# Differential attention: keys 0 to 511 of the two softmaxes' addition as an accumulating transfer

## What is computed

```
Q, K = X Wq + bq, X Wk + bk            # 2 x 64 columns a head
A1 = Q1 K1^T / 8 ; A2 = Q2 K2^T / 8    # 1024 x 1024 a head and batch
P  = softmax(A1) - lam * softmax(A2)
O  = P V ;  Y = concat(O) Wo + bo
out = x + 0.2 * layernorm(Y) * gamma + ... + ffn(x)
```

## Time and profile before

| | |
|---|---|
| median of 3 runs | 1207.48 us (1206.95 to 1208.09) |
| the profiled execution | 1207.97 us |
| its span, first to last instruction | 1206.2 us |
| TensorE busy | 1168.2 us, 97% |
| GpSimd busy | 1017.3 us, 84% |
| ScalarE busy | 968.9 us, 80% |
| VectorE busy | 905.6 us, 75% |
| mean granted TensorE clock | 0.99 |
| moved by DMA | 63.41 MB, mean 53 GB/s |

### The profile page before, as it was taken

One profiled execution on the slowest core, in us unless ns is written; L12 is line 12 of the kernel. 1 busy time (PEld: TensorE's weight loads), 2 busy tenths in 40 slices (PEclk: granted clock), 3 DMA queues, 4 the chain that ended last, 5 costly groups with the idle time before them and its releaser, 6 DMA issues.

```text
span 1206.2 us, 28081 instructions
## 1 busy us (share of the span) xinstructions
PE 1168.2 (97%) x9730; PEld 841.2 (70%) x9730; DVE 905.6 (75%) x1573; ACT 968.9 (80%) x1711; POOL 1017.3 (84%) x657
## 2 busy tenths in 40 slices
PE   5899999999999999999999999999999999998998
PEld 4666767666677776767676767676767776765797
DVE  8878878786787878887878887877887877874510
ACT  3398888887888888988888988888888888985432
POOL 3599999999999999999999999999999999989000
PEclk8999999999999999999999999999999999997999
DMA  8832211221112111222221112221112221110000
GB/s 208 312 80 51 50 44 49 49 49 42 23 39 49 49 49 44 49 49 49 49 49 40 30 34 49 49 49 43 49 49 49 49 49 42 25 28 1 1 18 18
DMA packets 74134, 63.41 MB, mean 53 GB/s; under 512 B 45172, under 2 KB 63092, under 8 KB 74100
## 3 DMA queue, kind: packets, MB, share of 16 engines
q1 hardware_dynamic: 73092, 62.78, 20.3%
q10 hardware_dynamic: 880, 0.19, 0.1%
q0 software_dynamic: 128, 0.01, 0.0%
HBM read 19.96 MB, written 9.44 MB: 24 GB/s over the span
## 4 chain that ended last, share of the span: by engine, by line
PE 75%; POOL 19%; DVE 4%; issue 1%; ACT 0%; DMA 0%; DVEq 0%; SPq 0%; POOLq 0%; ACTq 0%
PE ps L517 24%; PE ps L533 18%; PE ps L547 16%; POOL p_mix L431 11%; PE ps L472 7%; POOL work L428 5%; PE ps L559 4%; PE ps L611 3%; PE ps L598 2%; PE ps L499 1%; DVE pt L862 1%; DVE small L906 1%; POOL wqk_lo L343 1%; POOL w L406 0%; POOL wqk_hi L340 0%
## 5 line engine op out<-in xcount | busy, mean ns | idle before, releaser
L906 DVE TENSOR_REDUCE small<-ps 128x1 f32<-128x1024 f32 x512 | 613.8, 1220 | 114.6 <-PE ps L517 113.9
L431 POOL TENSOR_TENSOR p_mix<-p_mix,work 128x1024 f32<-128x1024 f32 x256 | 609.0, 2379 | 21.4
L533 PEld LDWEIGHTS ps<-ident,p_mix 64*128 64x128 f32 x4096 | 309.6, 139 | 191.7 <-issue 168.1
L725 ACT ACTIVATE pt<-ps 128x512 f32<-128x512 f32 x512 | 305.6, 597 | 131.2 <-PE ps L533 120.7
L533 PE MATMUL ps<-ident,p_mix 64*128 64x64 f32 x4096 | 352.6, 226 | 15.7 <-POOL p_mix L431 11.2
L428 POOL TENSOR_SCALAR work<-work,small 128x1024 f32<-128x1024 f32 x256 | 307.1, 1200 | 42.8 <-DVE small L931 42.8
L712 ACT ACTIVATE p_mix<-ps,small 128x1024 f32<-128x1024 f32 x256 | 284.8, 1113 | 15.4 <-DVE small L906 15.3
L712 ACT ACTIVATE work<-ps,small 128x1024 f32<-128x1024 f32 x256 | 284.4, 1111 | 12.5 <-DVE small L906 12.5
L547 PE MATMUL ps<-pt,v_h 128*64 128x512 f32 x1024 | 248.7, 606 | 0.0
L517 PE MATMUL ps<-k_hi,q_hi 64*128 64x512 f32 x512 | 234.4, 458 | 3.7 <-ACT p_mix L712 1.7
L517 PE MATMUL ps<-k_hi,qx_hi 64*128 64x512 f32 x512 | 230.5, 450 | 0.0
(11 more groups left out here) (135 smaller groups left out, 1305.3 us busy)
## 6 DMA issues: line engine op xcount, KB each, us to landing
qx_hi<-q_hi SPq DMA_DIRECT2D x64, 256.0 KB, 3.7
qx_lo<-q_lo SPq DMA_DIRECT2D x64, 256.0 KB, 4.6
v_scratch<-pt SPq DMA_DIRECT2D x16, 512.0 KB, 3.5
v_h<-v_scratch SPq DMA_DIRECT2D x32, 256.0 KB, 2.9
wqk_raw<-in_L_attn_Wk SPq DMA_DIRECT2D x31, 64.0 KB, 1.7
wqk_raw<-in_L_attn_Wq SPq DMA_DIRECT2D x31, 64.0 KB, 1.9
wo_dup<-in_L_attn_Wo SPq DMA_DIRECT2D x2, 512.0 KB, 7.1
w_raw<-in_L_ffn_W1e SPq DMA_DIRECT2D x4, 256.0 KB, 3.2
```

The source lines that it names most:

```text
L431: pool.tensor_tensor(e1, e1, e2, ALU.add).then_inc(mix_done, 1)
L533: mm = pe.transpose(pt_ps[:, c * D:(c + 1) * D], p_mix[rows, col:col + P], ident[rows, rows])
L725: act.activation(pt4[:, kb % 2, :, j * P + half * D:j * P + (half + 1) * D], pt_ps.rearrange("p (c q) -> p c q", c=KC), ACT.Copy).then_inc ...
L906: dve.tensor_reduce(neg_max[:, m:m + 1], slot[SLOT[k, s]], AX.X, ALU.max, negate=True)\
```

## The change

Of the addition of a row (1024 keys, 128 partitions) the first 512 columns become a transfer that GpSimd issues right after the scaling, with an accumulate operation: it reads e2 and e1 and writes e1, 256 KB of each. GpSimd itself adds the other 512 columns. Each of the four buffers has its own semaphore (`mix_landed`), raised by 16 when its transfer has landed. TensorE, before it transposes a row, and ScalarE, before it overwrites a buffer of `work`, wait for that and for `mix_done` (`mix_ready`).

```diff
--- before.py
+++ after.py
@@ -150,12 +150,22 @@
         s_ready, max_done, exp_done = sem("s_ready"), sem("max_done"), sem("exp_done")
         recip_done = sem("recip_done")
         scaled, mix_done = sem("scaled"), sem("mix_done")
+        mix_landed = [sem(f"mix_landed{i}") for i in range(4)]
         pt_ready, pt_evac = sem("pt_ready"), sem("pt_evac")
         pv_done, o_evac, y_mm, y_evac = sem("pv_done"), sem("o_evac"), sem("y_mm"), sem("y_evac")
         w1_split, h_mm = sem("w1_split"), sem("h_mm")
         h_done, out_mm, f_out = sem("h_done"), sem("out_mm"), sem("f_out")
         y_started, lny, lny_sqrt = sem("y_started"), sem("lny"), sem("lny_sqrt")
         stored = sem("stored")
+
+        def mix_ready(eng, g, k):
+
+
+            if k < 0:
+                g, k = g - 1, k + BODY
+            if not isinstance(g, int) or g >= 0:
+                eng.wait_ge(mix_landed[k % 4], 16 * (g * (BODY // 4) + k // 4 + 1))
+                eng.wait_ge(mix_done, g * BODY + k + 1)
 
         def after(eng, s, count):
 
@@ -428,7 +438,8 @@
                     pool.tensor_scalar(e2, e2, l_inv[:, 2 * km + 1:2 * km + 2], l1_neg[:, km % 4:km % 4 + 1],
                                        ALU.mult, ALU.mult).then_inc(scaled, 1)
                     pool.wait_ge(scaled, n)
-                    pool.tensor_tensor(e1, e1, e2, ALU.add).then_inc(mix_done, 1)
+                    pool.dma_start(e1[:, 0:S // 2], e2[:, 0:S // 2], accum_op=ALU.add).then_inc(mix_landed[km % 4], 16)
+                    pool.tensor_tensor(e1[:, S // 2:], e1[:, S // 2:], e2[:, S // 2:], ALU.add).then_inc(mix_done, 1)
                 if k % TB == SPLIT_W_AT and now(g, k, -2 * TB):
                     split_w(g * 2 + k // TB + 2)
                 set_expert(n)
@@ -523,7 +534,7 @@
 
                 n = g * BODY + k - LAG
                 if half == 0:
-                    pe.wait_ge(mix_done, n + 1)
+                    mix_ready(pe, g, k - LAG)
                 after(pe, pt_evac, 2 * n + half)
                 pe.nop(nofuse=True)
 
@@ -707,7 +718,7 @@
                 if s == 0:
                     after(act, pt_ready, 2 * (n - 3))
                 else:
-                    after(act, mix_done, n - 3)
+                    mix_ready(act, g, k - 4)
                 m, l = (k % 2) * 2 + s, (k % 4) * 2 + s
                 act.activation((p_mix, e2_buf)[s][:, k % 4 * S:(k % 4 + 1) * S], slot[SLOT[k, s]], ACT.Exp,
                                bias=neg_max[:, m:m + 1], scale=1.0, accum_out=l_sum[:, l:l + 1])\
```

## The result

The changed kernel takes **1293.47 us** (median of 4 runs, 1291.27 to 1293.62) against 1207.22 of the kernel before on the same chip: ratio 1.069, 95% interval 1.067 to 1.072. The prediction was 1282, within 1205 to 1410. The profiled execution is the 1291.27 us one.

What follows compares the result with a forecast made beforehand. The prediction took TensorE to set the pace, with GpSimd holding a small reserve. To the profiled 1207.97 us it added 63 (fourth-row stalls) + 12 (collisions) + 1 (extra waits) - 2 (tail) = +74: 1282 us, range 1205 to 1410.

Steps and rivals of the forecast that it cites:

- the prediction's own signs: In the changed profile: landing about 4.8 us after issue, some 63 third-step waits of 1 us; wrong if landing below 3.8.
- The landing: Accumulating 256 KB transfer on GpSimd's queue: 4.8 us from start of issue until TensorE is released, against room of 3.8.
- +63: Fourth row of each block of four: TensorE's transposition stalls 1.0 us for the landing, over 63 blocks, in us.
- GpSimd's row: GpSimd's work per row, scaling, issue and half addition: falls from 3.64 to 3.24 us, taking the split out of the way.
- The collisions: Third and fourth rows' transfers beside SyncE's q crossing and v load: 0.4 us per eight rows, 31 times, +12 us.
- The first eight rows: Start of the run: the first block was called unlike the others, and nothing was taken for it.
- The extra wait: One more semaphore wait per row on TensorE's and ScalarE's sequencers, hidden behind queued matmuls: +1 us, at most 13.
- The tail: Last rows, where GpSimd is the bound: some five rows save 0.4 us each, -2 us.
- The clock: TensorE's granted clock in the loop: 1.00 throughout, so no part of the sum.
- Rival 1: Transfer before the transposition: hidden if it takes at most 3.75 us, so faster, 1197 to 1206, say 1203 us; chance 0.15.
- Rival 2: GpSimd's issue is dear and GpSimd becomes the bound: at 2.0 us an issue, +205, 1413 us; chance 0.10.
- rival 3: DMA engines add more slowly than they copy: at 7.1 us a transfer, +208, 1416 us; chance 0.12.

Runs made afterwards that it cites:

- e4: Changed kernel with the 512-column transfer as a plain copy over e1 instead of an accumulation: 1229.05 us, ratio 1.017.
- e7: Changed kernel with the whole 1024-column addition as the transfer, GpSimd only issuing it: 1364.73 us, ratio 1.129.
- e6: Changed kernel with SyncE's q_lo crossing moved one row pair later, one transfer after the other, and the v load to the next block: 1260.99 us.
- e9: Changed kernel with q_lo's crossing and v load drawn apart, plus GpSimd alone adding the fourth row behind the weight split: 1232.96 us.
- e10: Changed kernel with no transfer in the row meeting the crossing and the row behind the weight split; GpSimd adds those alone: 1227.44 us.
- e3: Changed kernel with the accumulating transfer carrying 16 columns instead of 512: 1234.74 us, ratio 1.022.
- e5: Kernel before with one more, always met, semaphore wait on TensorE ahead of each row's transposition: 1213.43 us against 1207.61.

## Why the prediction came out right, and which steps were wrong

The direction was right, and 1282 is 11 us from the measured 1293, but the sum got there with wrong parts, and that it came so close is luck. The forecast that 8 in 10 of the loss was a landing too long for every fourth row is refuted. By the prediction's own signs the mechanism failed: it called itself wrong if the landing was below 3.8 us, and it was 3.3; it wanted some 63 waits of 1 us, all in the third step of a block, and there were 43, most of them for the third row, in the second step.

- **The landing, taken as 4.8 us, is 3.3.** The base was too high: the 3.0 us came from SyncE's 64-partition transfers, while on GpSimd's queue 256 KB over 128 partitions land in 2.3 (e4). The added operand cost 1.0 where the prediction booked 1.8. So the **+63** for 63 fourth rows is 0 for most: 7 of 46 in the steady loop wait. The rule behind it (one stall a block for what the landing exceeds the room) holds where the landing does exceed the room: e7 shows its 1.0 us, with collisions and a clock loss on top that no term held.
- **GpSimd's row, taken as 3.24 us, is 3.65, as before.** In the rows above it is 1.47 of scaling, where the prediction had 1.20, a gap of 0.30 for the issue's wait on the scaling's semaphore, where the addition's had been 0.08, 0.62 from the issue to the half addition, as taken, and 1.26 from there to the next scaling. So the weight split still delays the fourth row behind it, which the prediction had reasoned away: 1.1 us per eight rows where nothing covers it (e6 against e9).
- **The collisions, booked as +12, are the main item.** The prediction named the third row, the 1 MB and a landing of 7 us against a room of 6.4, and measured landings of 6.8 and 6.9 agree. It then took 0.4 us of the possible stall per eight rows. In fact the room was 5.8 us, because the issue came at GpSimd's old pace, and TensorE lost 1.5 us there in the mean. e10, without transfers in this row and the one behind the split, brings back 2.1 of the 2.5 us per eight rows.
- **The first eight rows, taken as 0, are +9.7.** Experts' weights, q and v are loaded there, and the first five landings took 5.0 to 7.6 us; the longest wait of TensorE, 4.8 us, is among them. Of the 9.7 us 5.3 stay with transfers of 8 KB (e3), whose first four landings still took 4.2 to 5.1.
- **The extra wait, taken as +1, is +5.8** (e5); the upper bound was 13. It hides where the prediction said, except ahead of the fourth row of each block.
- **The tail, taken as -2, is 0**: 37.1 us both times; its premise was the cheaper row.
- **The clock, taken as no part of the sum, is one.** Of the 23 eight-row stretches of the steady loop 15 keep clock 1.00 and take 34.9 us on average, 8 have 0.95 and take 36.0. How much of that 1.1 is the clock and how much the longer stall that lowered it was not separated.

Rival 1, the hidden transfer, came closer than its chance said: the lone landing of 3.3 us is under its point of 3.75. It failed because a landing among other traffic is another matter, and because the fourth row behind the split has less room than that. From the rule of the Trainium skill, "DMA: Bandwidth & Descriptors", section "Anatomy of one DMA", 2.6 us for 256 KB, the prediction had estimated near 3.2 with the issue, and 3.3 was measured. But the plain copy that the rule describes landed 2.3 us after the start of its issue, so the two errors, a plain copy taken too slow and no price for the adding, nearly cancel. Rival 2 (a dear issue) and rival 3 (slow adding in the DMA engines) did not occur: the issue shows 0.88 us, and adding 256 KB cost 1.0.

## What to carry to other kernels

A transfer put into a steady loop should be judged in each of its slots, not by its median: here six of eight slots were almost free, and two, one beside the loop's bulk loads and one behind other work of the issuing engine, cost 2.1 us of 2.5 per eight rows. When one of two stalls in a period is taken away, look whether the other appears before calling it a failure. And half an addition moved off an engine need not relieve it: the issue and its wait took here what the half saved.

## What the runs showed that was not expected

- An accumulation has a price apart from moving bytes: on GpSimd's queue 2.3 us for a plain 256 KB, 3.3 for an accumulating one, 4.6 for 512 KB, 2.0 for 8 KB.
- GpSimd pauses before some issues for a time no semaphore explains. In the changed kernel (scaling, then the issue with the pause before it):

```profile
560.10 1.49 POOL L438 TENSOR_SCALAR work<-work,small 128x1024 f32<-128x1024 f32 x1
563.23 0.89 POOL L441 DMA_DIRECT2D p_mix<-work  x1 [1.63 <-issue]
```

  It is 1.01 us before transfers 60, 117, 174 and 231 (57 apart) and 1.63 before 113 and 223 (110 apart), counted from 0, and at the same counts with 16, 512 or 1024 columns; where some rows have no transfer, the counts of transfers stay the same within one. With the plain copy only 113 and 223 have it, at 2.97 us. It goes by the number of transfers, not by their bytes; what it is was not tried.
- In e7, behind 24 of 46 waits of 1.2 to 2.7 us, TensorE was granted half its clock for some microseconds. Over the steady loop this cost about half as much as the waits themselves.
- A semaphore wait that is always met cost TensorE nothing at six rows of eight and 0.1 to 0.15 us at the two that are transposed between the two score tiles of a step (e5).
